# Score matmuls of a causal attention: 64-row contraction against zero-padded keys over 128 rows

## What is computed

```
x = x + 0.5 * ffn(layernorm(x))      # silu(x Wup^T) * (x Wgate^T), then Wdown^T; ternary weights; 1024 hidden
x = x + attention(layernorm(x))      # 16 heads of 16, rotary embedding, causal softmax, output projection
x = x + 0.5 * ffn(layernorm(x))
```

## Time and profile before

| | |
|---|---|
| median of three runs | 969.17 us (969.09 to 969.97) |
| profiled execution: span | 966.7 us |
| around the span (median less span) | 2.5 us |
| TensorE busy, 7488 matmuls | 791.4 us, 82% |
| VectorE busy | 742.8 us, 77% |
| ScalarE busy | 637.3 us, 66% |
| GpSimd busy | 552.8 us, 57% |

### The profile page before, as it was taken

How to read it: one execution, slowest core, us unless ns; L and a number is a source line. 1 busy time by engine, 2 the same in 40 slices (tenths; PEclk the granted TensorE clock), 3 DMA queues, 4 the chain that set the end, 5 groups by cost and what they waited for, 6 DMA issues and landing times.

```text
span 966.7 us, 21146 instructions
## 1 busy us (share of the span) xinstructions
PE 791.4 (82%) x7488; PEld 601.0 (62%) x7488; DVE 742.8 (77%) x1640; ACT 637.3 (66%) x1349; POOL 552.8 (57%) x535
## 2 busy tenths in 40 slices
PE   1347879898987989888987989888999899878866
PEld 0235657676765767666765776666777767656544
DVE  3644577989895898869895898959888988867653
ACT  2113677877776787757776787857777778767542
POOL 1037565666664676746664675746676666644221
PEclk9959889999998999989998999989999999989687
DMA  8300000000000000000000000000000000000000
GB/s 304 95 1 1 1 1 1 2 13 1 13 1 4 12 2 12 2 14 1 13 1 4 12 2 12 3 14 1 13 1 13 1 13 2 12 1 13 1 12 12
DMA packets 9964, 15.30 MB, mean 16 GB/s; under 512 B 640, under 2 KB 9088, under 8 KB 9344
## 3 DMA queue, kind: packets, MB, share of 16 engines
q1 hardware_dynamic: 9280, 11.54, 3.5%
q10 hardware_dynamic: 576, 2.29, 0.6%
HBM read 9.63 MB, written 4.19 MB: 14 GB/s over the span
## 4 chain that ended last, share of the span: by engine, by line
issue 26%; POOL 21%; PE 21%; DVE 20%; ACT 10%; DMA 1%; POOLq 0%; DVEq 0%; SPq 0%; ACTq 0%
POOL hid_l L1032 5%; POOL prob_l L1025 4%; PE misc_ps L387 3%; POOL rope_s L1004 3%; PE up_ps L387 2%; PE down_ps L387 2%; PE misc_ps L499 2%; ACT prob L641 2%; POOL rope_c L1003 2%; PE probt_ps L452 2%; POOL rstd L982 2%; PE score_ps L406 2%; DVE neg_max L873 2%; PE pv_ps L434 2%; DVE silu_b L928 2%
## 5 line engine op out<-in xcount | busy, mean ns | idle before, releaser
L1032 POOL TENSOR_TENSOR hid_l<-hid,hid_h 128x512 f16<-128x512 f32 x128 | 148.7, 1162 | 267.0 <-ACT hid_h L656 259.3
L632 ACT ACTIVATE prob_h<-probt_ps 128x384 f16<-128x384 f32 x256 | 127.4, 498 | 118.0 <-PE probt_ps L452 116.0
L1025 POOL TENSOR_TENSOR prob_l<-prob_t,prob_h 128x384 f16<-128x384 f32 x128 | 117.9, 921 | 70.3 <-ACT prob_t L636 69.8
L641 ACT ACTIVATE prob<-score_ps,exp_bias,exp_scale 128x256 f32<-128x256 f32 x256 | 146.8, 573 | 1.8 <-DVE exp_bias L879 1.6
L452 PE MATMUL probt_ps<-ident_f,prob 128*128 128x128 f32 x768 | 135.0, 287 | 13.0 <-ACT prob_t L636 13.0
L387 PE MATMUL up_ps<-xt_hi,tern_up 128*128 128x256 f16 x512 | 129.2, 289 | 19.5 <-DVE tern_up L711 12.4
L387 PE MATMUL down_ps<-tern_down,hid_h 128*128 128x256 f16 x512 | 121.8, 277 | 19.5 <-POOL hid_l L1032 19.4
L387 PE MATMUL up_ps<-xt_lo,tern_up 128*128 128x256 f16 x512 | 129.2, 289 | 0.0
L873 DVE TENSOR_REDUCE neg_max<-score_ps 128x2 f32<-128x512 f32 x128 | 87.7, 685 | 53.3 <-PE score_ps L408 53.0
L387 PE MATMUL gate_ps<-xt_hi,tern_gate 128*128 128x256 f16 x512 | 125.9, 284 | 1.8 <-DVE tern_gate L711 1.8
L928 DVE SCALAR_TENSOR_TENSOR silu_b<-tanh_b,up_ps 128x512 f32<-128x512 f32 x128 | 87.2, 681 | 52.1 <-ACT tanh_b L650 52.0
(11 more groups left out here) (108 smaller groups left out, 1990.7 us busy)
## 6 DMA issues: line engine op xcount, KB each, us to landing
xs<-x SPq DMA_DIRECT2D x16, 256.0 KB, 2.8
out<-xs SPq DMA_DIRECT2D x16, 256.0 KB, 2.1
raw_gate<-w_gate_t ACTq DMA_DIRECT2D x1, 1024.0 KB, 7.5
raw_up<-w_up_t SPq DMA_DIRECT2D x1, 1024.0 KB, 7.7
raw_down<-w_down_t SPq DMA_DIRECT2D x1, 1024.0 KB, 10.4
raw_w<-wqkvo ACTq DMA_DIRECT2D x1, 1024.0 KB, 12.5
cos<-rope_cos SPq DMA_DIRECT2D x1, 512.0 KB, 13.7
sin<-rope_sin SPq DMA_DIRECT2D x1, 512.0 KB, 14.4
```

The costliest lines, as they stand in the source:

```text
L632: act.activation(prob_h[:, pair % 2, j, :], probt_ps[:, 0:384], ACT.Copy).then_inc(prob_h_done, 1)
L641: act.activation(prob[:, s % 2, j, 0:256], score_ps[:, j, 0:256], ACT.Exp, bias=exp_bias[:, j:j + 1], scale=exp_scale[:, :])
L1025: pool.tensor_tensor(prob_l[:, pair % 2, 0, :], prob_t[:, pair % 2, :], prob_h[:, pair % 2, 0, :], ALU.subtract).then_inc(prob_l_done[0], 1)
L1032: pool.tensor_tensor(hid_l[:, s % 2, :, :].rearrange("p m n -> p (m n)"), hid[:, s % 2, :], hid_h[:, s % 2, :, :].rearrange("p m n -> p (m ...
```

## The change

The keys get a buffer with one plane per head, `k_pad`, as wide as `q_stk` but with both heads' planes. It is zeroed once by GpSimd at the start. The plane of the first head keeps zeros in partitions 64 to 127, that of the second in 0 to 63. The copy of each key stack is then two copies over 64 partitions each, and L406 and L408 take all 128 partitions of q against the plane of their head. The zeros take the other head's q out of the sum. Nothing else is changed; the orders of the slots are the same.

```diff
--- before.py
+++ after.py
@@ -254,7 +254,7 @@
         q_row = sb("q_row", [P, NT, HEADS, 4, HD], F16)
         k_row = sb("k_row", [P, NT, HEADS, 4, HD], F16)
         q_stk = sb("q_stk", [P, 2, SLOTS, SEQ], F16)
-        k_stk = sb("k_stk", [P, 2, SLOTS, SEQ], F16)
+        k_pad = sb("k_pad", [P, 2, SLOTS, 2, SEQ], F16)
         v_row = sb("v_row", [P, 2, NT * HEADS, VW], F16)
 
 
@@ -291,6 +291,7 @@
         abs_done, abs_all, tern_done = sem("abs_done"), sem("abs_all"), sem("tern_done")
         wmax_done, wmax_all, split_done = sem("wmax_done"), sem("wmax_all"), sem("split_done")
         casts_done, ones_done = sem("casts_done"), sem("ones_done")
+        pad_zeroed = sem("pad_zeroed")
         scales_done, w_scales_done = sem("scales_done"), sem("w_scales_done")
         below_done = sem("below_done")
 
@@ -328,11 +329,21 @@
 
         def copy_stack(engine, st, name, lag, copy):
 
+
             tile = int(name[-1])
-            stk = q_stk if name.startswith("stack_q") else k_stk
+            par = (st.first - lag) % 2
+            cols = slice(tile * P, (tile + 1) * P)
+            src = misc_h16[:, :].rearrange("p (s n) -> p s n", n=P)
             engine.wait_ge(misc_written, st.at(lambda t: misc_through(t, name)))
-            copy(stk[:, (st.first - lag) % 2, :, tile * P:(tile + 1) * P],
-                 misc_h16[:, :].rearrange("p (s n) -> p s n", n=P)).then_inc(misc_taken, 1)
+            if name.startswith("stack_q"):
+                copy(q_stk[:, par, :, cols], src).then_inc(misc_taken, 1)
+                return
+            if st.first == lag:
+                engine.wait_ge(pad_zeroed, 1)
+            for j in range(2):
+                half = slice(STK * j, STK * (j + 1))
+                c = copy(k_pad[half, par, :, j, cols], src[half])
+            c.then_inc(misc_taken, 1)
 
         def row_lo(engine, st, tile, m):
 
@@ -401,8 +412,8 @@
                     pe.wait_ge(exp_done[j], st.at(lambda t: SLOTS * (t - 2) + s))
                     pe.matmul(score_ps[:, j, P:3 * P], ident_b[:, :], mask_b[:, :], start=True, stop=False,
                               skip_group_check=True)
-                    q = q_stk[STK * j:STK * (j + 1), par, s, :]
-                    k = k_stk[STK * j:STK * (j + 1), par, s, :]
+                    q = q_stk[:, par, s, :]
+                    k = k_pad[:, par, s, j, :]
                     pe.matmul(score_ps[:, j, 0:2 * P], q[:, P:2 * P], k[:, 0:2 * P], start=False, stop=True,
                               skip_group_check=True)
                     mm = pe.matmul(score_ps[:, j, 2 * P:3 * P], q[:, 0:P], k[:, 0:P], start=False, stop=True,
@@ -1065,6 +1076,8 @@
                 pool.wait_ge(wmax_done, 1)
                 pool.partition_all_reduce(w_max_all[:, :], w_max[:, :], P, RMAX).then_inc(wmax_all, 1)
 
+            pool.memset(k_pad[:, :, :, :, :].rearrange("p a s j n -> p (a s j n)").bitcast(F32), 0.0
+                        ).then_inc(pad_zeroed, 1)
             pool.wait_ge(casts_done, 1)
             run_steps(pool, step, before={0: sum_all})
 
```

## The result

The changed kernel takes 962.64 us, the median of four runs (960.95 to 964.65), against 969.57 us for the kernel before in four runs beside it (969.09 to 970.35). The ratio is 0.993, with a 95% interval of 0.9909 to 0.995. The gain is real, 6.9 us, and about 60% of what I forecast.

The account below looks back on a forecast made before the run. TensorE was taken to bound slots 0 to 3 of a full step, VectorE slots 3 to 7. Span 966.7 less 23.0 saved plus 11.3 added gave 955.0, with 2.5 around it 957.5 us; range 948 to 970.

Parts of the forecast that it names:

- score pairs, steps 3 to 15: In the 13 full steps, cheaper score pairs in slots 0 to 3 save 1.19 us a step, 15.5 us.
- rest of steps 3 to 15, loop turns among it: Four slots behind a loop turn, at half clock: the pair gives 0.40 instead of 0.21, 0.8 us more saved.
- first score, steps 1, 2, 16, 17, tail: Outside full steps: 24 pairs of steps 2, 16, 17 save 6.7 us (0 to 9.8); extra copies add 3.5.
- What a pair costs: Two heads' score matmuls on TensorE: 128 rows throughout cut 0.96 us to 0.55, saving 0.41 (nothing to 0.45).
- Rival B: Excess is not from row height: pairs stay at 0.96 us, only the copies show, 980.5 us; chance 5%.
- Where it reaches the end: Saving per full step: 0.21, 0.41, 0.21, 0.36 us in slots 0 to 3, none in slots 4 to 7.
- Rival A: VectorE becomes the bound in slots 0 to 3 too, so 15.5 us are lost: 973 us; chance 13%.
- stack_k0: Second half copy on VectorE adds 0.60 us a step (0.3 to 0.68), fully paid: 7.8 us over 13 steps.
- rival C: Each pair at the ends gives 0.41 us and the added copies are hidden by half: 948.7 us; chance 11%.
- stack_k1: Second half copy on ScalarE, 1.03 us more, covered by waits and 0.60 us slack: cost 0, up to 13.4.
- Start, steps 1, 2 and 16: Extra copies in these steps add 3.5 us (none to 4.9); GpSimd's first memset is hidden, 0, up to 4.
- Slots 4 to 7: 0: Score savings there give 0, since the product with v waits for VectorE's L921, which scores do not feed.

Follow-up runs that it names:

- rows alone: Changed kernel with each key stack copied once into the first plane, both heads' scores over 128 rows of it (second head's keys left out): 942.82 us, ratio 0.9725.
- copies alone: Changed kernel with its planes, memset and double key copies kept, but score matmuls back on 64 rows: 978.97 us, ratio 1.0127 to the kernel before.
- same fillers: Dummy matmuls added to each kernel, 8 in slot 3's wait and 6 in slot 4's: changed kernel 942.21 us, kernel before 956.09 us.

## Why the prediction was right or wrong

The sum by its own terms, in us of the span. "Measured" is from the slot table and the sections, in one profiled execution of each kernel.

```
term                                        predicted   measured
score pairs, steps 3 to 15 (13 x)             -15.5      -15.0   13 x 1.15, rows alone
both key copies, steps 3 to 15 (13 x)          +7.8       +3.8   13 x 0.29
falls of the clock behind slot 3               none       +8.4   7 more, 1.2 each
rest of steps 3 to 15, loop turns among it     -0.8       +0.3   to make up 689.1 -> 686.6
first score, steps 1, 2, 16, 17, tail          -3.2       -3.4   +2.0 +0.0 -3.7 -1.7
sum                                           -11.7       -5.9
```

In the row of the rest, the turns are 0.6 us shorter each (18.8 to 18.2), but one slot 6, in step 13, takes 8.59 us instead of 7.70, and the last two slots of step 15 are 1.3 us longer. Why is open.

- *What a pair costs.* Right: 0.54 us for 0.55, by both signs that it named, the distance of 0.11 and the load ahead of its matmul. Rival B is out, and so is the rule of the Trainium skill ("TensorE: Matmul & The Clock Gate", Part 3) that would have ended there: at 128 rows throughout, loads run beside matmuls in flight.
- *Where it reaches the end.* Right: 0.20, 0.42, 0.21 and 0.31 for 0.21, 0.41, 0.21 and 0.36, and nothing in slots 4 to 7. In slot 3 the saving was cut off as the row for VectorE's wait said. Rival A is out: slots 0 to 3 are all shorter, by 1.36 us in all.
- *stack_k0.* Mis-sized. It was to be paid with 0.60 us, because VectorE is the bound there; row maximum did come 0.81 later, and 0.23 came through. What failed is the step "the stretch where VectorE is the bound: 13 x 0.60 = 7.8 us, fully paid". That VectorE was full did not mean that its instructions had their own lengths: one of them was 0.6 us longer than alone, beside GpSimd, and moving it past GpSimd's instruction gave that back. Full busy time contains blocked time. This half of rival C, copies hidden by half, came true.
- *stack_k1.* The chain was right: hid_h came 0.68 late and GpSimd's rows of the second norm 0.70, as forecast. The slack was mis-sized. I took the 0.60 us from the end of L993 to the start of L499 as free, but the transposes cannot follow the rows at once: they now start 0.15 us behind them (468.04, 468.19). So 0.24 of the 0.70 came through where I had 0.10, and slot 7 grew by 0.27. The cover that I named at L402 of slot 0 held and gave back 0.21. The net is 0.06, and the zero was close.
- *Start, steps 1, 2 and 16.* The memset took 3.51 us, inside 0 to 8.3, and moved the sum over the weights by 1.85 us, of which 0.24 reached the first copy of the stack (92.25 to 92.49); the zero was about right. In step 1 TensorE waits 2.14 us for the copies, where it waited 1.11. Rows alone against after has the first score 3.1 us later and step 2 3.0 longer, steps 16 and 17 0.7 shorter: 5.4 us for the copies outside the full steps, against 3.5, a bit over my bound of 4.9. Against that stands more saved outside the full steps than the 6.7: rows alone give 1.1 at the first score, 3.0 in step 2, 3.0 in steps 16 and 17 and 1.7 in the tail, 8.8 us. That the tail is 1.7 us shorter I cannot attribute: it is as short with the copies alone, where no score changed.
- *The step that is missing.* I priced what stays unused on an engine off the bound at nothing: "Slots 4 to 7: 0", and of the scores "they end before it". TensorE's freed time became waiting (0.90 to 1.00 us and 0.55 to 0.86) in a place where the clock had already fallen twice in the kernel before, and the seven more falls took 8.4 us. I had also let step 9 stand for all 13 full steps, and in the kernel before steps 7 and 13 have a slot 4 of 6.65 and 6.71 us. The page before does not give them away. Its clock row dips in the loop only at the four turns, and a fall is short against a slice of 24 us:

```profile
PEclk9959889999998999989998999989999999989687
```

Only the cut of every step into its slots shows them. The question to ask of every saving beside another engine's bound was: what does TensorE do with it.
- *Luck.* Without the seven more falls the span would have been 14.3 us shorter, more than forecast. The 4.0 us too much that I had put on the copies stands against the 8.4 us of falls, of which I knew nothing. That the sum came out as near as 5.1 us is in part this.

That falls cost the changed kernel about 10 us is shown: with work in the wait of slot 3 they are gone, with the same work in slot 6 they stay, and the two differ by 8.5 us. With the same fillers on both kernels there are no falls in either and 13.9 us between them. Some of that is the turns: 15.9 us each with the kernel before (14.2 to 18.0), 14.9 with the changed one, 4 us in all, so 10 us are left for the change proper. What is *not* settled is how many falls a kernel gets, and so whether the change itself brought the seven more. The two profiled kernels with 64-row scores and no fillers had 2 and 0. Kernels with 128-row scores and nothing in the waits of slots 3 and 4 had 9, 3, 7, 8, 2 and 12 in the profiled executions (in the order told above), with the same two waits in slots 3 and 4, and the time of one kernel moves with it from run to run (the one with the late memset: 959.44 us at a mean granted clock of 0.928, 969.54 at 0.917). That longer waits bring more falls fits these numbers and is not shown by them; the two of the kernel before may have been a lucky number. What was seen every time is that the four kernels with slot 3 filled had none, in 52 steps.

## What to carry to other kernels

Where TensorE is the bound, padding a 64-row contraction to the full height pays if row heights alternate: 0.1 us for each switch, here 0.42 a pair, against the price of filling the padded planes (9.5 us here, by the copies alone). Before counting a saving on TensorE, look where it goes: in slots where another engine is the bound it lengthens waits, and behind two waits of about 1 us close together, in a kernel otherwise busy, the clock can fall and take a good part of what was saved, here 8.4 of 14.3 us. A handful of dummy matmuls in the wait is then worth trying, as a test and as a remedy: 20 us here, about half of it from the falls and the rest from shorter loop turns. And measure slack up to where the next engine could really start, not up to where it did.

## What was not expected of the hardware

- A fall of TensorE's clock in the middle of the loop, for over 3 us at 0.50, behind two waits of 1.00 and 0.86 us with 1.2 us of work between, which did not come in any of 52 steps with 8 matmuls in the first wait.
- TensorE's stops at the loop turn, 2.43 and 2.01 us, change with the body: with 8 or 14 more matmuls in any of the places tried, the two slots around a turn are some 3 us shorter on average, and the second stop is gone at all 20 turns. What TensorE stops for is open.
- VectorE's 128x4 scaling lasts 0.82 us beside GpSimd's 1.04 us instruction and 0.23 alone; a cast lasts 3.79 us beside GpSimd's memset of 4096 words a partition (3.51 us).
- GpSimd's sum over the partitions came 1.85 us later with a memset of 3.51 us ahead of its first norm, though that norm ended only 0.09 us later; the idle time between grew from 8.84 us to 10.59. With the memset later it is 9.49. Why is open.
